# Folding the experts' first bias into the second through the second layer's weights

## What is computed

```python
x_mixed = _mix(x, mix_kernel)
h = jnp.einsum('bsd,pdm->bspm', x_mixed, W1) + b1          # W1 (9, 512, 128), b1 (9, 128)
stacked_paths = jnp.einsum('bspm,pmd->bspd', h, W2) + b2   # W2 (9, 128, 512), b2 (9, 512)
scores = jnp.tanh(x_mixed @ Wo1 + bo1) @ Wo2 + bo2
idx = jnp.argmax(scores, axis=-1)
...
return _layernorm(x + collapsed, gamma, beta)              # collapsed: the chosen expert's row
```

## Time and profile before

| | us |
|---|---|
| median of 3 runs | 752.56 |
| the three runs | 751.38, 752.56, 755.74 |
| the profiled execution | 751.71 |
| its span, first to last instruction | 749.9 |
| PE busy (matmul) | 708.2 (94%) |
| DVE busy | 375.8 (50%) |
| ACT busy | 339.7 (45%) |
| POOL busy | 197.7 (26%) |

### The profile page before, as it was taken

How to read it: one execution, slowest core, us unless ns; L and a number is a source line. 1 busy time by engine, 2 the same in 40 slices (tenths; PEclk the granted TensorE clock), 3 DMA queues, 4 the chain that set the end, 5 groups by cost and what they waited for, 6 DMA issues and landing times. The chain is left out here.

```text
span 749.9 us, 20567 instructions
## 1 busy us (share of the span) xinstructions
PE 708.2 (94%) x8150; PEld 550.0 (73%) x8150; DVE 375.8 (50%) x993; ACT 339.7 (45%) x743; POOL 197.7 (26%) x281
## 2 busy tenths in 40 slices
PE   4999999999999999999999999998999989788994
PEld 3777787787788778778778778786787777564662
DVE  5455334424424424425334434576568777581675
ACT  3535534535435434444444443543354544541663
POOL 0001001001001001001000011048776775535755
PEclk9999999999999999999999999999999999989997
DMA  8211110110110110110110211251000005348930
GB/s 332 86 56 58 58 50 9 58 56 0 56 56 0 56 56 0 56 56 0 56 56 5 51 56 38 75 136 10 17 15 28 29 31 199 103 164 303 347 137 31
DMA packets 17557, 55.97 MB, mean 75 GB/s; under 512 B 6098, under 2 KB 6354, under 8 KB 14566
## 3 DMA queue, kind: packets, MB, share of 16 engines
q1 hardware_dynamic: 13926, 40.64, 15.9%
q0 software_dynamic: 3584, 14.69, 5.1%
HBM read 46.93 MB, written 10.49 MB: 77 GB/s over the span
## 5 line engine op out<-in xcount | busy, mean ns | idle before, releaser
L96 PE MATMUL pj<-W_both 128*128 128x512 f32 x544 | 222.1, 408 | 10.1 <-DVE W_both L595 10.0
L98 PE MATMUL pj<-W_both 128*128 128x512 f32 x544 | 213.8, 393 | 0.0
L97 PE MATMUL pj<-W_both 128*128 128x512 f32 x544 | 212.7, 391 | 0.0
L96 PEld LDWEIGHTS pj<-W_both 128*128 128x128 f32 x544 | 102.8, 189 | 43.2 <-issue 23.6
L98 PEld LDWEIGHTS pj<-W_both 128*128 128x128 f32 x544 | 102.6, 189 | 23.0
L236 POOL COPY q_b<-Q_T 128x128 f32 (+1 forms) x32 | 9.3, 290 | 416.3 <-PE tp L359 349.3
L97 PEld LDWEIGHTS pj<-W_both 128*128 128x128 f32 x544 | 103.0, 189 | 19.2
L493 ACT ACTIVATE K<-pj,bk 128x512 f32<-128x512 f32 x64 | 44.1, 689 | 136.4 <-PE pj L98 136.4
L654 DVE CUSTOM_DVE_ANT_0 m_flat<-sc,mask 128x257 f32<-128x257 f32 x64 | 24.7, 424 | 116.5 <-PE tp L359 95.2
L508 ACT ACTIVATE p_flat<-m_flat,nmax 128x257 f32<-128x257 f32 x128 | 63.8, 501 | 25.5 <-DVE nmax L654 25.4
L500 ACT ACTIVATE V<-pj 128x512 f32<-128x512 f32 x64 | 38.2, 596 | 73.3 <-PE pj L98 71.8
(11 more groups left out here) (365 smaller groups left out, 1149.7 us busy)
## 6 DMA issues: line engine op xcount, KB each, us to landing
raw<-ctx_dram SPq DMA_DIRECT2D x15, 1024.0 KB, 4.8
experts<-w_dram SPq DMA_DIRECT2D x6, 768.0 KB, 5.8
raw<-w_dram SPq DMA_DIRECT2D x4, 1024.0 KB, 4.9
x_nat<-x_dram SPq DMA_DIRECT2D x2, 1024.0 KB, 12.1
rows<-z3s SPq DMA_DIRECT2D x8, 256.0 KB, 2.0
rows<-x_nat SPq DMA_DIRECT2D x8, 256.0 KB, 3.1
rows<-xm SPq DMA_DIRECT2D x8, 256.0 KB, 2.2
raw<-wk_dram SPq DMA_DIRECT2D x2, 512.0 KB, 5.7
```

Source lines behind the costliest of these rows:

```text
L96: eng.matmul(out, a_hi, b_hi, start=first, stop=False)
L97: eng.matmul(out, a_lo, b_hi, start=False, stop=False)
L98: return eng.matmul(out, a_hi, b_lo, start=False, stop=last)
```

## The change

`hidden(k)` loses its bias product; the first of its four products now starts the accumulation. The first bias is put on the diagonal blocks of a wide zero tile `b1_apart` (128 x 9*41), so that the product of block e with expert e's second-layer weights lands in rows e and 32+e. Nine such fp32 products (`joint_biases`), accumulated in one PSUM bank, take the place of `idle(5)`. DVE adds the second bias to their sum and splits it into high and low part (`split_biases`, now four operations, now after `list_tokens`); `outputs(0)` waits for it. At the old place of `split_biases` stands `spread_b1` (a memset and two copies). SP loads b1 once, as it lies in memory, in place of twice turned. `biases` loses 128 columns. The gathers in flight ahead of the loop go from 10 to 9 (`LANDINGS`), with one semaphore less for them and one more for the biases; so the tenth gather moves into POOL's loop.

```diff
@@ -860,7 +860,8 @@
         to_slot, from_slot, none = sb("to_slot", [P, NS], I32), sb("from_slot", [P, NS], I32), sb("none", [P, NS])
         at = sb("at", [1, 2 * NS], I32)
         of_slot = sb("of_slot", [KB, NS], F32R)
-        b1_raw, biases = sb("b1_raw", [KB, P]), sb("biases", [KB, P + D], F32R)
+        b1, b1_apart = sb("b1", [P, E]), sb("b1_apart", [P, E * KB])
+        biases = sb("biases", [KB, D], F32R)
         total, mean, squares = sb("total", [P, NS]), sb("mean", [P, NS]), sb("squares", [P, NS])
         root_in, root, ln_eps = sb("root_in", [P, NS]), sb("root", [P, NS]), sb("ln_eps", [P, 1])
         variance_made = sem("variance_made")
@@ -882,7 +883,7 @@
                  raw[:, 0, 0:3 * D], raw[:, 1, 0:3 * D], x_flat[:, 0:3 * D], x_flat[:, 3 * D:6 * D],
                  bqkv[:, :, :].rearrange("p a n -> p (a n)"),
                  *(w[:, (3 + i) * 3 * D:(4 + i) * 3 * D] for w in (w1_all, w2_all) for i in range(3))]
-        AT_ONCE, LANDINGS = 7, 10
+        AT_ONCE, LANDINGS = 7, 9
         assert len(slots) == NS
 
         def slot(k, part):
@@ -908,6 +909,7 @@
         places = lists
         found = pw[0]
         map_bank, census_bank = pa[:, 2, :], pw[1]
+        joint_bank = pa[0:KB, 3, :]
 
         def last_bank(c):
             return pw[1] if c < 2 else pt[1]
@@ -928,6 +930,7 @@
             return pa[:, 2 + k % 2, :]
 
         tables, z_stored, xb_made, rows_in = sem("tables"), sem("z_stored"), sem("xb_made"), sem("rows_in")
+        biases_made = sem("biases_made")
         ex_in, exw_in = sem("ex_in"), sem("exw_in")
         (mix_made, g_done, th_made, gs_done, choice_made, step3, pos_done, places_made, placed_made, map_done,
          counted, found_pe, found_dve, rowsT_done, rows_out) = (
@@ -943,6 +946,7 @@
         stored = [sem(f"stored{i}") for i in range(NH)]
 
         TABLES = 18
+        SPREAD, JOINED = 1, 2
         LIFT = 1.5 * 2.0 ** 23 * P
         CENSUS, RANKS, SLOTS = 1, 2, 3
         USED, LISTED, GATHER, WEIGHTS, SCATTER = 1, 2, 3, 4, 5
@@ -990,11 +994,10 @@
             eng.wait_ge(wlo, 4)
             eng.wait_ge(wp_lo, 1)
             eng.dma_start(g_raw, io["wo1"].rearrange("p (c n) -> p c n", c=CT)).then_inc(ex_in, 16)
-            for name, dst in (("wo2", wo2[:, :]), ("bo1", bo1[:, :])):
+            for name, dst in (("wo2", wo2[:, :]), ("bo1", bo1[:, :]), ("b1", b1[:, :])):
                 eng.dma_start(dst, io[name]).then_inc(ex_in, 16)
             for r in (slice(0, E), slice(32, KB)):
                 eng.dma_start(b2_raw[r, :], io["b2"]).then_inc(ex_in, 16)
-                eng.dma_start(b1_raw[r, :], io["b1"].rearrange("m e -> e m"), allow_slow_non_contiguous=True).then_inc(ex_in, 16)
             eng.dma_start(bo2[:, :], row_on_all(io["bo2"])).then_inc(ex_in, 16)
 
             def load(i, layers=(0, 1)):
@@ -1391,7 +1394,7 @@
             def gate(g, cs=range(CT)):
                 a, b = GROUPS[g]
                 if g == 0 and 0 in cs:
-                    eng.wait_ge(ex_in, 8 * 16)
+                    eng.wait_ge(ex_in, 7 * 16)
                     eng.wait_ge(qk_out, 2 * NT)
                 if g == 1:
                     eng.wait_ge(qT_out, NT)
@@ -1463,11 +1466,15 @@
                     eng.matmul(found[0:1, (1 + i) * NS:(2 + i) * NS], weight_at[0:NB, i:i + 1], listed[:, :], start=True, stop=True)
                 eng.matmul(found[0:KB, 3 * NS:4 * NS], expert_of[0:NB, :], listed[:, :], start=True, stop=True).then_inc(found_pe, 1)
 
-            def idle(n):
+            def joint_biases():
 
                 eng.wait_ge(exw_in, 6 * 16)
-                for _ in range(n):
-                    eng.matmul(pa[:, 2, :], ident[:, :], w1_all[:, 0:D], start=True, stop=True)
+                eng.wait_ge(biases_made, SPREAD)
+                eng.wait_ge(rows_out, NT)
+                for e_ in range(E):
+                    mm = eng.matmul(joint_bank, b1_apart[:, e_ * KB:(e_ + 1) * KB], w2_all[:, e_ * D:(e_ + 1) * D],
+                                    start=e_ == 0, stop=e_ == E - 1)
+                mm.then_inc(found_pe, 1)
 
             def x_transposes(k):
                 eng.wait_ge(slot_in[k % len(slot_in)], 16 * (k // len(slot_in) + 1))
@@ -1483,10 +1490,9 @@
                 w_at = eng.value_load(at[0:1, NS + k:NS + k + 1], min_val=0, max_val=2 * 3 * D + 2 * P)
                 eng.wait_ge(xT_out, k + 1)
                 need(eng, h_out, k - 1)
-                eng.matmul(h_bank(k), of_slot[:, k:k + 1].broadcast_to([KB, P]), biases[:, 0:P], start=True, stop=False)
                 for c in range(CT):
                     mm = eng.matmul(h_bank(k), x_T(k)[:, c * P:(c + 1) * P], w1_all[:, bass.ds(w_at + c * 3 * P, P)],
-                                    start=False, stop=c == CT - 1)
+                                    start=c == 0, stop=c == CT - 1)
                 mm.then_inc(h_done, 1)
 
             def h_transpose(k):
@@ -1497,8 +1503,10 @@
             def outputs(k):
                 w_at = eng.value_load(at[0:1, k:k + 1], min_val=0, max_val=(E - 1) * D)
                 eng.wait_ge(hT_out, k + 1)
+                if k == 0:
+                    eng.wait_ge(biases_made, JOINED)
                 need(eng, mean_made, k - 1)
-                eng.matmul(y_bank(k), of_slot[:, k:k + 1].broadcast_to([KB, P]), biases[:, P:P + D], start=True, stop=False)
+                eng.matmul(y_bank(k), of_slot[:, k:k + 1].broadcast_to([KB, P]), biases[:, :], start=True, stop=False)
                 eng.matmul(y_bank(k), h_T(k), w2_all[:, bass.ds(w_at, D)], start=False, stop=True).then_inc(y_done, 1)
 
             steps(eng, body)
@@ -1548,7 +1556,7 @@
             ranks()
             map_tiles(3)
             slot_lists()
-            idle(5)
+            joint_biases()
 
             x_transposes(0)
             hidden(0)
@@ -1933,12 +1941,18 @@
             def split_biases():
 
                 hi, lo = slice(0, E), slice(32, KB)
-                eng.wait_ge(ex_in, 8 * 16)
-                for r in (hi, lo):
-                    ch3.link(eng.tensor_copy(biases[r, 0:P], b1_raw[r, :]))
-                    ch3.link(eng.tensor_copy(biases[r, P:], b2_raw[r, :]))
-                ch3.link(eng.tensor_tensor(biases[lo, 0:P], b1_raw[lo, :], biases[lo, 0:P].bitcast(F32), ALU.subtract))
-                ch3.link(eng.tensor_tensor(biases[lo, P:], b2_raw[lo, :], biases[lo, P:].bitcast(F32), ALU.subtract))
+                eng.wait_ge(found_pe, SLOTS + 1)
+                ch3.link(eng.tensor_tensor(biases[hi, :], joint_bank[hi, :], b2_raw[hi, :], ALU.add))
+                ch3.link(eng.tensor_tensor(b2_raw[lo, :], joint_bank[lo, :], b2_raw[lo, :], ALU.add))
+                ch3.link(eng.tensor_copy(biases[lo, :], b2_raw[lo, :]))
+                eng.tensor_tensor(biases[lo, :], b2_raw[lo, :], biases[lo, :].bitcast(F32), ALU.subtract).then_inc(biases_made, 1)
+
+            def spread_b1():
+
+                eng.wait_ge(ex_in, 7 * 16)
+                ch3.link(eng.memset(b1_apart[:, :], 0.0))
+                ch3.link(eng.tensor_copy(b1_apart[:, 0:(E - 1) * (KB + 1) + 1:KB + 1], b1[:, :]))
+                eng.tensor_copy(b1_apart[:, 32:32 + (E - 1) * (KB + 1) + 1:KB + 1], b1[:, :]).then_inc(biases_made, 1)
 
             def weight_offsets():
 
@@ -2052,7 +2066,7 @@
 
             def centre(k):
                 if k == 0:
-                    eng.wait_ge(ex_in, 9 * 16)
+                    eng.wait_ge(ex_in, 8 * 16)
                 eng.wait_ge(mean_made, k + 1)
                 need(eng, stored[k % NH], k // NH * 16)
                 ch3.link(eng.scalar_tensor_tensor(out=result(k), in0=slot(k, 1), scalar=mean[:, k:k + 1], in1=gamma,
@@ -2066,7 +2080,7 @@
             for it in range(NT):
                 body(it)
                 if it == 4:
-                    split_biases()
+                    spread_b1()
                 if it == 5:
                     weight_offsets()
             ch = Chain(eng, step, count["at"])
@@ -2107,6 +2121,7 @@
             mark_places((7,))
             list_blocks()
             list_tokens()
+            split_biases()
 
             for k in range(NS - 2):
                 residual(k)
```

## The result

| | before | changed |
|---|---|---|
| median, us | 751.40 (750.67 to 755.74, 6 runs) | 746.54 (745.99 to 749.11, 6 runs) |
| the same once more, later | 752.25 | 746.79 (742.24 to 748.26, 7 runs) |
| profiled execution, us | 751.71 | 745.99 |
| its span, us | 749.9 | 744.3 |

The ratio is 0.9932 with a 95% interval of 0.9907 to 0.9956; the repeat gives 0.9937 (0.9917 to 0.9957). So the change saves 0.7%, some 5 us. 747.9 us was forecast, and the range of 746.4 to 751.2 holds the median. But the highest chance, 0.53, stood on "within 0.5%", and that was the wrong case.

The account below looks back on a forecast made before the run. PE was taken to set the pace in the expert-slot loop (10.00 of 10 us busy). Start 1.5, loop -4.9 and self-attention -0.8 summed to -4.2 us, from 752.1 to 747.9 us; range 746.4 to 751.2.

Parts of the forecast that it names:

- within 0.5%: Whole kernel: a change under 3.8 us, not told from none; chance 0.53, against faster 0.42 and slower 0.05.
- upstream: Everything up to the first product of the slot lists, self-attention included; forecast 0.80 us saved.
- tail: From the eight passes of `hidden(15)` to the end of the span; no change forecast.
- The slot: Loop over expert slots: dropping the bias product saves 0.25 + 0.10 = 0.35 us a slot, 4.9 over 14.
- Rival B: Slot loop: bias product worth less, 0.25 or 0.11 us a slot, total 749.3 or 751.3; chance 0.17.
- 81 ns: Slot loop: the skill page's price for a 128-column product, giving 1.1 us over 14 slots, total 751.7.
- rival C: Slot loop: POOL's gather rounds of 3.36 us become the bound, 2.1 us lost, total 750.0; chance 0.10.
- The start: Before the slot loop: `joint_biases` takes 18 passes for `idle(5)`'s ten, costing 1.5 us, bounds 1.3 to 2.0.
- wait for DVE: At `outputs(0)`: PE's added wait for DVE's four split operations, claimed covered by 2.2 us, so costing nothing.
- Rival D: Joint product: all 18 passes at half clock, 1.6 us slower than before, 753.7; turns slower from ten; chance 0.10.
- The stall: Self-attention: PE's 0.80 us loss behind `split_biases` goes whole; bounds 0 and 0.8.
- rival E: Self-attention: PE's lost time stays or returns at the next wait, saving only 3.4 us, total 748.7; chance 0.08.

Follow-up runs that it names:

- fp32 run: Kernel before with the first-bias product in plain fp32 in place of fp32r: ratio 1.003 (1.0012 to 1.0048), slower, a slot of 3.53 us.
- 128-row runs: Bias products zero-padded from 41 to 128 rows: both in the kernel before, ratio 0.9918; the one left in the changed kernel, 0.9907; with two further edits, 0.9892.
- split-late run: Kernel before with `split_biases` moved from the self-attention to behind `list_tokens`, both bias products kept: ratio 0.9978 (0.9958 to 0.9998).

## Why the prediction was right or wrong

Forecast, and measured in the profiled pair, in us:

| stage | forecast | measured | repeat |
|---|---|---|---|
| upstream | -0.8 | -2.28 | -5.03 |
| start | +1.5 | +1.29 | +1.33 |
| loop | -4.9 | -5.60 | -5.89 |
| tail | 0 | +0.99 | +0.19 |
| sum | -4.2 | -5.6 | -9.4 |

The repeat is taken against the first trace of before. Its upstream figure is scatter for the greater part: by the medians the change is worth 4.9 us, and 5.5 in the repeat.

**The slot: right mechanism, one term too small.** I counted the gap ahead of the product and the product, 0.35. This is the step that failed: the loop's term of the sum, 14 x 0.35 = 4.9, in which the gap behind the product stood at nothing. That gap of 0.10 is in the earlier trace rows as well (eight passes in 1.09, where the earlier trace rows, by 0.43 for four transposes, would give 0.86), but part of those 0.23 stayed, and no row told which. By the changed kernel the price is 0.45 a slot, and the fourteen periods, 3.80, twelve of 3.37 and 2.92 before, give 0.35 + 12 x 0.45 + 0.44 = 6.2, of which 5.6 and 5.9 are left in the two traces. And I called the gap one ahead of the fp32r product; the fp32 run shows that the format isn't its cause, the 128-row runs that it goes when the 41 rows do. Rival B falls: nothing of the gaps moved to a neighbour. In the sentence apart I held the trace against the 81 ns of the Trainium skill ("TensorE: Matmul & The Clock Gate", section "Back-to-back issue gap"); the measured 0.45 us bear the trace out, for a product of 41 rows.

**POOL: rival C came true in part.** I took the round's 3.36 us from the earlier trace rows and 2.0 us of delay as covered by DVE's slack. The round itself can go at 3.13; the 3.36 was PE's pace. In the kernel before, POOL's root at 701.88 started 0.14 us after ACT had its input ready (701.74, the row below), so a wait lay within what the earlier trace rows shows without a pause:

```profile
701.44 0.30 ACT L1714 ACTIVATE root_in<-squares,ln_eps 128x1 f32<-128x1 f32 x1
```

Yet two of the changed kernel's six rounds took 3.5 and 3.7 us, so the delay came out at 2.6 us, near the 2.0 forecast. But the slack was counted on the root alone. What I overlooked is the ring of result buffers: a late scatter lands late, and DVE's `centre` of four slots on waits for it, then the residual behind it, then PE's bank. It took back 0.55 us (0.26 in the repeat), not the 2.1 of the rival. Why the tail grew by 0.99 (0.19 in the repeat) no run shows.

**The start: right.** +1.3 against 1.5: the lower end of my bounds. The joint product was 0.4 shorter than worked out, with three passes at half clock where the earlier trace rows has about four, `hidden(0)` took 0.99 us and not 1.09, and the wait for DVE never showed. Rival D is real as a cause and didn't decide: three to seven of 18 passes at half clock in the traces looked at, not the ten from which it turns.

**The self-attention: perhaps undersized.** The stall went whole, 0.85 for 0.80, and rival E falls. I stopped there. A further 0.2 at the next wait and the pause in the scores, 0.9 and 0.1 behind it, went as well; but the split-late run bounds the whole by its ratio only to 0.2 to 3.2 us, which holds 0.8. The pause could not have been forecast from any row that I can point to.

**The net and the chances.** Start, loop and tail sum to -3.3 in the pair, against -3.4: that is luck, two errors of opposite sign, the slot's price on one side and POOL and the tail on the other. In the repeat they sum to -4.4, and the slot's price shows. The short term did its harm in the last step, how the numbers follow: I put the bound of 0.5%, 3.8 us, against a forecast of 4.2 and laid 0.17 of its chance and nearly all of B, C and E within. I had bounded the terms that the rows left open as "at most this", though for two of them the rows gave no top: the gap behind the product, and what a stall in an iteration drags with it. With the slot at 0.45 alone the forecast would have been 5.6 and the largest chance on faster.

## What to carry to other kernels

When a small product seems dear, read the starts before and behind it, both; and before removing it, give its stationary tile the same rows as its neighbours': zeros cost no time here, and won as much as the algebra. When an engine at 10 of 10 gets work taken off, work out the next engine's own round without its waits, and follow every buffer ring that its late results close, not only the first reader.

## What was not expected of the hardware

- A product with 41 rows between ones with 128 cost its slot 0.45 us (0.25 for itself, 0.10 on each side); with both bias products padded with zeros to 128 rows, it took 0.14. The eight passes behind it went from 1.09 to 0.86, below even the changed kernel's 0.99: there the other bias product, also of 41 rows, still cost them, for with 128 rows in it they take as little as 0.83. Four transposes went from 0.53 to 0.36; without a bias product behind them they take 0.43 whatever the rows of the other. The loads around a tile of 41 rows start with their products, and with 128 rows ahead of them (727.68 for both, against 713.54 and 713.78). What in the 41 rows holds them back, no run shows.
- PE paused for 0.5 to 0.8 us at the 102nd of 128 equal small products in four of fourteen traces, with nothing that it waited for in the trace. Open.
- The square root on ACT cost one table load of 1.28 us inside the loop, once, from 695.63 us on; the ACTIVATE for which it was loaded started at 696.93, and PE's period grew by 0.04 us.
